# Fetching an expert layer's second-half result rows rank by rank, from before its last block pairs have run

## The chip, the core and the metric

The kernel runs on one core of one Trainium2 chip. The metric is the device time of one execution in microseconds (us). The engines are named as in the profile: PE (TensorE, matrix products; PEld is its weight load), DVE (VectorE), ACT (ScalarE), POOL (GpSimd) and SP (SyncE, which here only issues transfers). Each engine runs its own list of instructions strictly in the order in which it is written; the lists meet only at semaphores.

## What is computed

Two transformer layers over x [2048 tokens, 256], each an attention with 16 heads and a mixture-of-experts layer with 64 experts of which every token uses 8. The attention is not touched by the change except for some added transfers. The expert layer, cut to what matters:

```python
logits = x @ gate_w.T
topv, topi = jax.lax.top_k(logits, TOP_K)          # 8 of 64 experts for each token
rw = jax.nn.softmax(topv)
inter = silu(gate) * up                            # of the chosen experts
out = sum over the 8 chosen e of rw[e] * (inter[e] @ dp_w[e].T)
x = x + out + sh_g * sh_out                        # sh: a shared expert
```

The order in which the eight products of a token are added is free within rounding.

## The kernel before

**The tokens of an expert layer are worked in two halves** of 1024 (`HALVES`: tiles 8 to 15 of 128 tokens first, then tiles 0 to 7). A half has 8192 pairs of a token and an expert. They are sorted by expert into blocks of 128 rows, each block belonging to one expert, with 128 blocks for a half so that it fits whatever the routing; two blocks are a "pair", so a half is 64 pairs (`NPAIR`) and the layer 128 (`PAIRS`).

**The work of a pair n.** ACT copies the block's expert weights from `weights` to `fetched` ("fetch"); from pair 32 (`OTHER_FROM`) on DVE copies the second block's ("other"). PE multiplies (`gate_up`, L1393), ACT takes the silu (L1170), DVE the product with the other branch (L1858, two instructions), PE multiplies again (`down`, L1410), ACT moves the result out of its banks into one of two buffers `outs` (L1176), and SP writes that 256 KB to `expert_rows` in memory (L811). ACT waits before L1176 for the write of two pairs earlier (`outs_out`).

**Where tokens come from.** POOL issues all gathers of a layer in one list, `for m in range(GATHERS)`, 4 times 64 of 128 rows of 1 KB each, through `ring`, five buffers: 64 gathers of the first half's tokens, 64 of the second half's, which ACT lays down transposed in `tokensT`, then 64 gathers of result rows of the first half and 64 of the second (L1009). Result gather n serves one token tile t and one rank k: for each of 128 tokens the row that its k-th row number (`rows_of`) names. DVE multiplies it by the token's weight and adds it to x ("combine", L1872), in the order t by t, all 8 ranks of a tile one after the other. A gather waits until the combine five before it has emptied its buffer (`combined`). The ranks come from an instruction that takes the 8 largest of a token's row numbers, largest first: rank 0 is a token's last row in the blocks' order, rank 7 its first.

**What starts the result gathers.** The first gather of a half waits for the writes of all 64 pairs of that half. So the first half's gathers can run beside the second half's pairs, and the second half's cannot start before the last pair is written. DVE's combines of the second half come after its last work on the pairs.

**What sets the order.** `expert_plan` is a small planner: it has a stream of items for each kind of work with a cost and what each needs, always takes the item that could start first, and gives PE, ACT and DVE their lists. POOL's list is written by hand. Between tiles POOL computes the standard deviations for the next layer's normalisation (`inverse_std`, L947 and L949) when DVE has the statistics of a block of four tiles; DVE then writes the normalised tiles `xn` (L1903), which PE transposes (L1437) when the next phase begins. At that boundary SP loads the second layer's weights `w_raw` (L850), and POOL splits them.

**The attention before it** (`core_plan`) has 16 blocks; at the end of each ACT copies sums (L1234), and for each SP issues four small transfers of maxima (neg_hi, neg_lo) that the next products wait for.

## Time and profile before

| | us |
|---|---|
| median of 3 runs | 2178.72 |
| lowest and highest | 2177.01, 2202.41 |
| the profiled execution, its device time | 2182.6 |
| its span in the profile | 2179.9 |
| first attention | about 0 to 562 |
| first expert layer | about 562 to 1080 |
| second attention | about 1080 to 1700 |
| second expert layer | about 1700 to 2180 |

How to read it: the span is the profile's own measure of the core from first to last instruction; the device time lies 2.7 us above it. Busy times can lie beside each other, since the engines run at once. An instruction's idle time is what its engine waited just before it, with the engine or transfer that ended the wait. Over the span PE is busy 79%, DVE 69%, ACT 51% and POOL 32%.

### The profile page before, as it was taken

How to read it: one execution, taken by the hardware profiler on the slowest of the kernel's cores; microseconds unless marked ns; L12 is line 12 of the kernel's file. 1: busy time of each engine (PE TensorE's matmuls, PEld its weight loads, DVE VectorE, ACT ScalarE, POOL GpSimd, SP SyncE). 2: the span in 40 equal slices, each digit the busy share in tenths (PEclk: the TensorE clock that was granted, in tenths of full speed). 3: DMA queues.
4: the chain of work that ended last, by engine and by line, in shares of the span. 5: the costliest groups of instructions: out<-in, count | busy, mean ns of one | idle time of the engine just before them, and what ended most of it. 6: DMA issues, size and time to landing. Idle time of an engine off the chain costs nothing.

```text
span 2179.9 us, 36690 instructions
## 1 busy us (share of the span) xinstructions
PE 1716.5 (79%) x12464; PEld 1102.6 (51%) x12464; DVE 1501.5 (69%) x3241; ACT 1108.9 (51%) x1975; POOL 703.5 (32%) x778
## 2 busy tenths in 40 slices
PE   5799999999767777991096999999997677778920
PEld 4545454445545666771074454544456455667720
DVE  6588888884676834884555788888853777438843
ACT  2145858566355655760041457485672456556710
POOL 5000101001266454446740001010011564545456
PEclk9778989899879988995595679797896799999965
DMA  4640314000444544664235402231004345446643
GB/s 151 138 63 2 44 19 51 11 2 2 174 158 140 168 151 151 209 192 127 82 113 101 60 2 34 28 38 23 2 2 167 113 141 168 156 148 198 212 139 115
DMA packets 123276, 217.59 MB, mean 100 GB/s; under 512 B 16380, under 2 KB 92044, under 8 KB 118812
## 3 DMA queue, kind: packets, MB, share of 16 engines
q1 hardware_dynamic: 98520, 148.10, 25.1%
q0 software_dynamic: 24576, 67.14, 11.2%
q8 instruction: 106, 1.74, 0.4%
q14 instruction: 74, 0.61, 0.1%
HBM read 124.20 MB, written 90.46 MB: 98 GB/s over the span
## 4 chain that ended last, share of the span: by engine, by line
PE 55%; DVE 13%; POOL 7%; DMA 7%; issue 7%; ACT 5%; another core or an unknown queue 4%; SPq 1%; DVEq 0%; ACTq 0%; POOLq 0%
PE late_banks L1575 13%; PE late_banks L1533 11%; PE exp_banks L1561 7%; PE late_banks L1393 7%; POOL ring_t L1009 5%; PE exp_banks L1410 4%; DMA expert_rows<-outs_t 4%; PE late_banks L1426 3%; PE late_banks L1368 3%; DVE chunk_max_t L1974 3%; PE late_banks L1539 2%; PE exp_banks L1426 2%; DVE hot_t L1688 2%; DVE inter_t L1858 1%
## 5 line engine op out<-in xcount | busy, mean ns | idle before, releaser
L1225 ACT ACTIVATE probs_t<-exp_banks 128x1024 f32<-128x1024 f32 (+3 forms) x640 | 538.9, 896 | 348.1 <-PE exp_banks L1561 346.9
L1974 DVE TENSOR_REDUCE chunk_max_t<-late_banks 128x1 f32<-128x512 f32 (+1 forms) x960 | 603.0, 683 | 110.8 <-PE late_banks L1533 89.4
L1084 POOL TENSOR_SCALAR_AFFINE_SELECT probs_t<-probs_t 128x512 f32<-128x512 f32 x128 | 81.6, 638 | 873.0 <-ACT probs_t L1225 873.0
L1393 PE MATMUL late_banks<-tokensT_t,fetched_t 128*128 x2048 | 311.2, 298 | 26.0 <-ACT fetched_t L1153 14.0
L1575 PE MATMUL late_banks<-probs_t,values_t 128*32 128x512 f32 (+3 forms) x2560 | 322.1, 579 | 9.9 <-POOL probs_t L1084 9.5
L1004 POOL DMA_INDIRECT ring_t<-token_rows,index_t x256 | 255.4, 998 | 206.2 <-PE late_banks L1368 130.1
L1009 POOL DMA_INDIRECT ring_t<-expert_rows,rows_of_t x256 | 244.3, 954 | 201.9 <-DVE x_sb_t L1872 112.5
L1393 PEld LDWEIGHTS late_banks<-tokensT_t,fetched_t 128*128 128x128 f32 x2048 | 267.7, 204 | 58.2 <-issue 44.2
L1858 DVE TENSOR_TENSOR inter_t<-late_banks,silu_t 64x256 f32<-64x256 f32 x512 | 217.5, 425 | 103.3 <-ACT silu_t L1170 55.1
L1533 PE MATMUL late_banks<-contextT_t,Qp_t 50*128 50x512 f32 (+7 forms) x640 | 247.5, 531 | 23.9 <-DVE part_lo_t L1915 11.8
L1410 PE MATMUL exp_banks<-fetched_t,inter_t 64*128 64x128 f32 x2048 | 194.6, 311 | 41.3 <-DVE inter_t L1858 22.7
L1533 PE MATMUL late_banks<-Kp_t,Qp_t 50*128 50x512 f32 (+7 forms) x640 | 224.0, 474 | 1.9 <-DVE chunk_max_t L1974 0.9
L1176 ACT ACTIVATE outs_t<-exp_banks 128x512 f32<-128x512 f32 x256 | 152.3, 595 | 114.5 <-PE exp_banks L1410 41.6
L1872 DVE SCALAR_TENSOR_TENSOR x_sb_t<-ring_t,row_top_t,x_sb_t 128x256 f32<-128x256 f32 x256 | 122.4, 478 | 113.6 <-DMA ring_t<-expert_rows,rows_of_t 100.9
L1533 PEld LDWEIGHTS late_banks<-contextT_t,Qp_t 50*128 50x128 f32 (+1 forms) x640 | 117.8, 230 | 143.8 <-DVE chunk_max_t L1974 95.2
L1410 PEld LDWEIGHTS exp_banks<-fetched_t,inter_t 64*128 64x128 f32 x2048 | 143.7, 198 | 81.2 <-DVE inter_t L1858 34.5
L1533 PEld LDWEIGHTS late_banks<-Kp_t,Qp_t 50*128 50x128 f32 (+1 forms) x640 | 105.6, 205 | 131.4 <-DVE chunk_max_t L1974 99.3
L1848 DVE COPY fetched_t<-weights_t 128x384 f32 x192 | 84.1, 438 | 120.4 <-PE exp_banks L1410 56.3
L1153 ACT ACTIVATE fetched_t<-weights_t 128x384 f32 x320 | 158.9, 519 | 14.4 <-issue 12.7
L1561 PE MATMUL exp_banks<-Qp_t,contextT_t 52*128 52x512 f32 (+7 forms) x640 | 150.4, 442 | 15.6 <-DMA Qp_t<-neg_lo_t 11.7
L1368 PE MATMUL late_banks<-ident_t,ring_t 128*128 128x128 f32 x512 | 103.3, 312 | 75.4 <-ACT tokensT_t L1163 47.9
L1561 PE MATMUL exp_banks<-Qp_t,Kp_t 52*128 52x512 f32 (+7 forms) x640 | 148.4, 429 | 6.8 <-ACT probs_t L1225 4.8
(222 smaller groups left out, 2007.7 us busy)
## 6 DMA issues: line engine op xcount, KB each, us to landing
expert_rows<-outs_t SPq DMA_DIRECT2D x256, 256.0 KB
weights_t<-in_experts SPq DMA_DIRECT2D x8, 1728.0 KB, 13.8
Qp_t<-q_parts SPq DMA_DIRECT2D x36, 256.0 KB
weights_t<-in_experts SPq DMA_DIRECT2D x4, 2112.0 KB, 9.7
Kp_t<-k_parts SPq DMA_DIRECT2D x24, 256.0 KB
q_parts<-part_hi_t SPq DMA_DIRECT2D x16, 256.0 KB, 2.6
q_parts<-part_lo_t SPq DMA_DIRECT2D x16, 256.0 KB, 3.2
k_parts<-part_hi_t SPq DMA_DIRECT2D x16, 256.0 KB, 3.2
```

The source lines that it names most:

```text
L1004: pool.indirect_dma_start(ring[:, slot, :], None, token_rows[f][:, :], bass.IndirectOffsetOnAxis(ap=index[h][:, n:n + 1], axis=0))\
L1009: pool.indirect_dma_start(ring[:, slot, :], None, expert_rows[f][h][:, :], bass.IndirectOffsetOnAxis(ap=rows_of[:, t, k:k + 1], axis=0))\
L1153: act.activation(fetched[:, n % NFETCH, blk, :], weights[:, bass.ds(fetches[n][blk], EW)], ACT.Copy)\
L1225: act.activation(probs[:, e % NP, 2 * p:2 * p + 2, off:QB], exp_banks[sq % 2][:, :, off:QB], ACT.Exp, scale=D ** -0.5).then_inc(exp_done, 1)
L1368: last = pe.transpose(bank[:, k * P:(k + 1) * P], ring[:, slot, k * P:(k + 1) * P], ident[:, :])
L1393: last = pe.matmul(bank[:, blk * P:(blk + 1) * P], fetched[:, n % NFETCH, blk, k * P:(k + 1) * P], tokensT[:, bass.ds(starts_of[n][blk] + ...
L1410: last = pe.matmul(down_bank(n, side)[:, blk * P:(blk + 1) * P], inter[rows, n % 2, blk * P:(blk + 1) * P], fetched[rows, n % NFETCH, blk, ...
L1533: last = pe.matmul(bank[:, begin:end], Qp[s][rows, p, t * P:(t + 1) * P], Kp[s][rows, p, c * QB:c * QB + end - begin], start=True, stop=c < b)
L1561: last = pe.matmul(exp_banks[sq % 2][:, hh, off:QB], Kp[s][rows, p, j * P:(j + 1) * P], Qp[s][rows, p, b * QB + off:(b + 1) * QB], start=T ...
L1575: last = pe.matmul(pv_banks[n % NPV][32 * h:32 * h + 32, off:QB], values[:, j, GH * g + h, :], probs[:, e % NP, h, off:QB], start=(j == 0) ...
L1858: dve.tensor_tensor(inter[side * EI:(side + 1) * EI, n % 2, :], up, silu[0:EI, n % 2, :], ALU.mult)\
L1974: op = dve.tensor_reduce(chunk_max[:, slot, p, r, c], bank[:, 0:n].rearrange("q (p k) -> q p k", p=len(parts)), AX.X, ALU.max)
```

## The change

1. The shared list on POOL loses its last 64 gathers (`GATHERS = 3 * NG`). They come in a list of their own, `LATE`: first ranks 7 to 3, each for all eight tiles (40 gathers), then ranks 2 to 0 for tiles 0 to 3 and for tiles 4 to 7 (24).
2. They land in `tokensT` (the last in `ring`), in places that the pairs have read by then: late gather i waits for the product `gate_up` of pair 96 + i // 2. There is no waiting for a combine between them.
3. A rank k of the first five waits for as many writes as the furthest row of that rank needs: `marks`, 8 numbers that DVE and PE work out from the row numbers (one transpose, one product, six small DVE instructions), and that POOL reads into registers. The 41st gather waits for all writes.
4. DVE combines them after its last work on the pairs, after normalising the first half's tiles, by groups of four gathers (one semaphore for four), each tile's ranks now eight or four instructions apart.
5. In the second half ACT copies both blocks' weights for every third pair (`BOTH_EVERY`), DVE the second block's for the other two. The planner no longer has the late combines, and has the row numbers and marks earlier in DVE's list; pair 21's `down` waits for the marks.
6. Both layers' second-half results lie in one tensor, `last_rows_out`, which ACT fills during the first attention with 16 transfers of 1 MB, one after each block's sums; SP waits for them before the expert layer's loads.
7. The second layer's weights are loaded after the 26th late combine, no longer after the last pair, and POOL splits them after the last combine.

```diff
-GATHERS = 4 * NG
+GATHERS = 3 * NG
+LATE_STEP, LATE_GROUP, LOADED_FROM = 3, 4, 26
...
+BOTH_EVERY = 3
...
+def both_copied(n):
+
+    return n < OTHER_FROM or n >= NPAIR and n % BOTH_EVERY == 0
+
+
+def late_order():
+
+    order = [(t, k) for k in range(TOPK - 1, LATE_STEP - 1, -1) for t in HALVES[1]]
+    for b in range(HT // TPB):
+        order += [(t, k) for k in range(LATE_STEP - 1, -1, -1) for t in HALVES[1][b * TPB:(b + 1) * TPB]]
+    return order
+
...
-    map_steps += [("index_out", 1), ("places", 1), ("table_out", 1)]
-    pieces = [("shares", 0)]
-    for h in range(2):
-        pieces += [("rows", h)] + [("weights", i) for i in range(h * PIECES, (h + 1) * PIECES)]
+    map_steps += [("index_out", 1), ("places", 1), ("table_out", 1), ("rows", 1), ("last_rows", 1), ("marks", 1)]
+    pieces = [("shares", 0), ("rows", 0)] + [("weights", i) for i in range(2 * PIECES)]
...
-               ("dve", [("other", n) for n in pairs if n >= OTHER_FROM]),
-               ("dve", [("combine", n) for n in range(2 * NG)]),
+               ("dve", [("other", n) for n in pairs if not both_copied(n)]),
+               ("dve", [("combine", n) for n in range(NG)]),
...
-                yield "table_out", 1, 0.0
+                yield "marks", 1, 0.0
...
-        expert_rows = [[nc.dram_tensor(f"expert_rows{f}{h}", [NBLK * P, E], F32).ap() for h in range(2)] for f in range(2)]
+        last_rows_out = nc.dram_tensor("last_rows_out", [NBLK * P, E], F32).ap()
...
+        def late_tile(i):
+
+            at = i % KC * (SLOTS + P) + i // KC * E
+            return tokensT[:, at:at + E] if i < NG - 1 else ring[:, 0, :]
...
+            sp.wait_ge(rows_set, 16 * len(BLOCKS))
...
-                    sp.wait_ge(down_done, layer * PAIRS)
+                    sp.wait_ge(combined, layer * 2 * NG - NG + LOADED_FROM)
...
+            pool.wait_ge(rows_ready, 2 * f + 2)
...
+            pool.wait_ge(marked, f + 1)
...
+            written = [*low_marks, *high_marks]
+            for i, (t, k) in enumerate(LATE):
+                if i in LATE_NORMS:
+                    inverse_std(pool, norm_of["f", f] + 1, LATE_NORMS[i])
+                pool.wait_ge(gate_up_done, f * PAIRS + NPAIR + NPAIR // 2 + i // 2 + 1)
+                if i == NG - 1:
+                    pool.wait_ge(combined, f * 2 * NG + NG)
+                if i < (TOPK - LATE_STEP) * HT:
+                    if i % HT == 0:
+                        for out in outs_out:
+                            pool.wait_ge(out, written[k])
+                elif i == (TOPK - LATE_STEP) * HT:
+                    for out in outs_out:
+                        pool.wait_ge(out, 16 * ((f + 1) * PAIRS // NOUT))
+                pool.indirect_dma_start(late_tile(i), None, expert_rows[f][1][:, :],
+                                        bass.IndirectOffsetOnAxis(ap=rows_of[:, t, k:k + 1], axis=0))\
+                    .then_inc(late_in[i // LATE_GROUP], 16)
+            for place in range(2, NB):
                 inverse_std(pool, norm_of["f", f] + 1, place)
 
...
+                if layer == 1:
+                    pool.wait_ge(combined, layer * 2 * NG)
...
-                    for blk in range(2 if n < OTHER_FROM else 1):
+                    for blk in range(2 if both_copied(n) else 1):
...
+                        if layer == 0:
+                            rows = slice(n * NBLK * P // len(BLOCKS), (n + 1) * NBLK * P // len(BLOCKS))
+                            act.dma_start(last_rows_out[rows, :].rearrange("(p r) e -> p (r e)", p=P),
+                                          values[:, 0:TPB, :, :].rearrange("p t h d -> p (t h d)")).then_inc(rows_set, 16)
...
+                        pe.wait_ge(mark_step, 5 * f + 3)
...
-                    if n == NG + 16:
-                        dve.wait_ge(down_done, (f + 1) * PAIRS)
-                        for b in MIDDLE[0:2]:
-                            normalise(phase, b)
+            dve.wait_ge(down_done, (f + 1) * PAIRS)
+            for b in MIDDLE[0:2]:
+                normalise(phase, b)
+            dve.wait_ge(weights_done, 2 * f + 2)
+            last = {}
+            for i, (t, k) in enumerate(LATE):
+                n = f * 2 * NG + NG + i
+                if i % LATE_GROUP == 0:
+                    dve.wait_ge(late_in[i // LATE_GROUP], 16 * LATE_GROUP * (f + 1))
+                if t in last:
+                    dve.wait_ge(combined, last[t])
+                dve.scalar_tensor_tensor(out=x[:, t, :], in0=late_tile(i), scalar=weight8[:, t, k:k + 1],
+                                         in1=x[:, t, :], op0=ALU.mult, op1=ALU.add).then_inc(combined, 1)
+                last[t] = n + 1
+                if k == 0 and t % TPB == TPB - 1:
+                    dve.wait_ge(combined, n + 1)
+                    statistics(phase, t // TPB)
```

**POOL's list where the second half's results are gathered** (first expert layer). Before, the second half's gathers follow the first half's in the ring, with the two lines of a standard deviation between them:

```order
L1009 DMA ring_t<-expert_rows,rows_of_t 128x256 [waits combined] x59
L1009 DMA ring_t<-expert_rows,rows_of_t 128x256 [waits outs_out1,combined,outs_out0,rows_ready]
L1009 DMA ring_t<-expert_rows,rows_of_t 128x256 [waits combined] x7
L947 TENSOR_SCALAR var_eps_t<-mean_var_t 128x4 [waits aggr_done]
L949 TENSOR_TENSOR rstd_t<-var_eps_t,minus_half_t 128x4 [waits eps_done]
L1009 DMA ring_t<-expert_rows,rows_of_t 128x256 [waits combined] x4
L947 TENSOR_SCALAR var_eps_t<-mean_var_t 128x4 [waits aggr_done]
L949 TENSOR_TENSOR rstd_t<-var_eps_t,minus_half_t 128x4 [waits eps_done]
L1009 DMA ring_t<-expert_rows,rows_of_t 128x256 [waits combined] x32
L947 TENSOR_SCALAR var_eps_t<-mean_var_t 128x4 [waits aggr_done]
```

Of the change, the same place: the 64 first-half gathers stay, the register loads follow, and the late gathers wait for pairs (`gate_up_done`) and not for combines.

```order
L1056 DMA ring_t<-expert_rows,rows_of_t 128x256 [waits combined] x59
L1061 TENSOR_LOAD silu_t [waits marked,rows_ready]
L1064 TENSOR_LOAD silu_t
L1081 DMA tokensT_t<-last_rows_out,rows_of_t 128x256 [waits outs_out1,outs_out0,gate_up_done]
...
L1081 DMA tokensT_t<-last_rows_out,rows_of_t 128x256 [waits outs_out1,outs_out0,gate_up_done]
L1081 DMA tokensT_t<-last_rows_out,rows_of_t 128x256 [waits gate_up_done] x22
L1081 DMA ring_t<-last_rows_out,rows_of_t 128x256 [waits combined,gate_up_done]
L997 TENSOR_SCALAR var_eps_t<-mean_var_t 128x4 [waits aggr_done]
```

What moved: nothing of the second half waits behind a combine any more, except its last gather; two of the four standard deviations now stand behind all gathers.

**DVE's list early in the second half** (about pairs 70 to 73; L1858 of before and L1977 of the change are the pair's product, COPY the weight copy, SCALAR_TENSOR_TENSOR the combine). Before, a copy and one combine stand between two products:

```order
L1872 SCALAR_TENSOR_TENSOR x_sb_t<-ring_t,row_top_t,x_sb_t 128x256
L1858 TENSOR_TENSOR inter_t<-late_banks,silu_t 64x256 x2
L1843 TENSOR_LOAD silu_t
L1848 ISA
L1848 COPY fetched_t<-weights_t 128x384
L1872 SCALAR_TENSOR_TENSOR x_sb_t<-ring_t,row_top_t,x_sb_t 128x256
L1858 TENSOR_TENSOR inter_t<-late_banks,silu_t 64x256 x2
L1848 ISA
L1848 COPY fetched_t<-weights_t 128x384
L1872 SCALAR_TENSOR_TENSOR x_sb_t<-ring_t,row_top_t,x_sb_t 128x256
L1858 TENSOR_TENSOR inter_t<-late_banks,silu_t 64x256 x2
```

Of the change, five combines and two copies stand in three pairs:

```order
L1977 TENSOR_TENSOR inter_t<-late_banks,silu_t 64x256 x2
L1967 ISA
L1967 COPY fetched_t<-weights_t 128x384
L1991 SCALAR_TENSOR_TENSOR x_sb_t<-ring_t,row_top_t,x_sb_t 128x256 x2
L1977 TENSOR_TENSOR inter_t<-late_banks,silu_t 64x256 x2
L1991 SCALAR_TENSOR_TENSOR x_sb_t<-ring_t,row_top_t,x_sb_t 128x256 x2
L1962 TENSOR_LOAD silu_t
L1967 ISA
L1967 COPY fetched_t<-weights_t 128x384
L1977 TENSOR_TENSOR inter_t<-late_banks,silu_t 64x256 x2
L1991 SCALAR_TENSOR_TENSOR x_sb_t<-ring_t,row_top_t,x_sb_t 128x256
L1977 TENSOR_TENSOR inter_t<-late_banks,silu_t 64x256 x2
```

What moved: the first half's 64 combines are spread over pairs 68 to 107, where they were spread over pairs 68 to 128.

**DVE's list at the end of the first expert layer.** Before:

```order
L1895 BN_AGGR mean_var_t<-stats_t 128x2 x4
L1872 SCALAR_TENSOR_TENSOR x_sb_t<-ring_t,row_top_t,x_sb_t 128x256 x17
L1903 TENSOR_SCALAR xn_t<-x_sb_t,mean_var_t,rstd_t 128x256 x8
L1872 SCALAR_TENSOR_TENSOR x_sb_t<-ring_t,row_top_t,x_sb_t 128x256 x15
L1892 BN_STATS stats_t<-x_sb_t 128x6 x4
L1895 BN_AGGR mean_var_t<-stats_t 128x2 x4
L1872 SCALAR_TENSOR_TENSOR x_sb_t<-ring_t,row_top_t,x_sb_t 128x256 x32
L1892 BN_STATS stats_t<-x_sb_t 128x6 x4
L1895 BN_AGGR mean_var_t<-stats_t 128x2 x4
L1903 TENSOR_SCALAR xn_t<-x_sb_t,mean_var_t,rstd_t 128x256 x8
```

Of the change (L2007 is the late combine, L2035 the normalisation of eight tiles, L2024 and L2027 the statistics):

```order
L1967 COPY fetched_t<-weights_t 128x384
L1977 TENSOR_TENSOR inter_t<-late_banks,silu_t 64x256 x6
L2035 TENSOR_SCALAR xn_t<-x_sb_t,mean_var_t,rstd_t 128x256 x8
L2007 SCALAR_TENSOR_TENSOR x_sb_t<-tokensT_t,row_top_t,x_sb_t 128x256 x52
L2024 BN_STATS stats_t<-x_sb_t 128x6 x4
L2027 BN_AGGR mean_var_t<-stats_t 128x2 x4
L2007 SCALAR_TENSOR_TENSOR x_sb_t<-tokensT_t,row_top_t,x_sb_t 128x256 x11
L2007 SCALAR_TENSOR_TENSOR x_sb_t<-ring_t,row_top_t,x_sb_t 128x256
L2024 BN_STATS stats_t<-x_sb_t 128x6 x4
L2027 BN_AGGR mean_var_t<-stats_t 128x2 x4
L2035 TENSOR_SCALAR xn_t<-x_sb_t,mean_var_t,rstd_t 128x256 x8
L2045 TENSOR_TENSOR xT_t<-exp_banks,xT_t 128x512 x4
L2045 TENSOR_TENSOR xT_t<-late_banks,xT_t 128x512 x4
```

What moved: the first half's normalisation stands ahead of all 64 late combines, and no combine of them stands beside a pair.

## Rows read from the trace of the kernel before

**Rows 1.** Busy time and rates by stretch; share of DMA engines and GB/s last.

```profile
core 0: us, PE busy (x) PEld busy (x) DVE busy (x) ACT busy (x) POOL busy (x), PEclk, DMA share, GB/s
100.00:560.00 460.00, 440.24 (x3194) 218.43 (x3191) 368.82 (x709) 277.75 (x340) 43.31 (x68) 0.88 0.17 23
1160.00:1700.00 540.00, 509.68 (x3448) 262.20 (x3448) 407.37 (x834) 295.85 (x376) 53.91 (x88) 0.82 0.23 41
857.00:978.00 121.00, 107.29 (x928) 90.86 (x928) 99.06 (x241) 78.44 (x174) 60.96 (x64) 0.94 0.64 196
990.00:1075.00 85.00, 3.67 (x16) 3.27 (x16) 34.12 (x78) 2.40 (x4) 65.36 (x70) 0.52 0.37 113
```

**Rows 2.** One line's instructions (ns min/median/max, first and last start): gathers, four stretches; DVE's copy.

```profile
L1009 POOL DMA_INDIRECT ring_t<-expert_rows,rows_of_t x64: 943/947/1142, 857.4 to 977.2; - x64
...
L1009 POOL DMA_INDIRECT ring_t<-expert_rows,rows_of_t x64: 945/949/1170, 990.4 to 1074.3; - x64
...
L1009 POOL DMA_INDIRECT ring_t<-expert_rows,rows_of_t x64: 943/947/1141, 1964.3 to 2082.2; - x64
...
L1009 POOL DMA_INDIRECT ring_t<-expert_rows,rows_of_t x64: 945/949/959, 2093.4 to 2172.4; - x64
...
L1848 DVE COPY fetched_t<-weights_t x60: 360/472/572, 857.8 to 980.8; 128x384 f32 x60
```

**Rows 3.** The silu, one for each pair, in four stretches of second halves.

```profile
L1170 ACT ACTIVATE silu_t<-late_banks x40: 360/378/380, 858.2 to 940.1; 64x256 f32<-64x256 f32 x40
...
L1170 ACT ACTIVATE silu_t<-late_banks x21: 362/378/379, 941.8 to 982.9; 64x256 f32<-64x256 f32 x21
...
L1170 ACT ACTIVATE silu_t<-late_banks x39: 361/378/379, 1968.5 to 2042.7; 64x256 f32<-64x256 f32 x39
...
L1170 ACT ACTIVATE silu_t<-late_banks x22: 360/378/380, 2042.7 to 2087.6; 64x256 f32<-64x256 f32 x22
```

**Rows 4.** Groups by line, 870 to 977 us: busy us, mean ns, idle before, releasers.

```profile
L1858 DVE TENSOR_TENSOR inter_t<-late_banks,silu_t 64x256 f32<-64x256 f32 x108 | 45.9, 425 | 13.1 <-ACT silu_t L1170 9.3 <-issue 1.9
L1176 ACT ACTIVATE outs_t<-exp_banks 128x512 f32<-128x512 f32 x54 | 32.2, 596 | 27.6 <-DMA expert_rows<-outs_t 15.5 <-PE exp_banks L1410 10.1 <-issue 1.9
L1872 DVE SCALAR_TENSOR_TENSOR x_sb_t<-ring_t,row_top_t,x_sb_t 128x256 f32<-128x256 f32 x55 | 25.8, 470 | 0.1
```

**Rows 5.** Timeline (start, us, engine, line), end of the first expert layer, then of the second.

```profile
1016.78 2.67 DVE L1903 TENSOR_SCALAR xn_t<-x_sb_t,mean_var_t,rstd_t 128x256 f32<-128x256 f32 x8
...
1077.04 0.48 DVE L1872 SCALAR_TENSOR_TENSOR x_sb_t<-ring_t,row_top_t,x_sb_t 128x256 f32<-128x256 f32 x1 [0.83 <-DMA ring_t<-expert_rows,rows_of_t]
1077.56 1.41 DVE L1892 BATCH_NORM_STATS2 stats_t<-x_sb_t 128x6 f32<-128x256 f32 x4
...
2175.19 0.49 DVE L1872 SCALAR_TENSOR_TENSOR x_sb_t<-ring_t,row_top_t,x_sb_t 128x256 f32<-128x256 f32 x1 [0.80 <-DMA ring_t<-expert_rows,rows_of_t]
```

**Rows 6.** The chain of waits, pieces in order of time: writes of result rows.

```profile
941.35 4.64 DMA expert_rows<-outs_t
...
987.38 2.20 DMA expert_rows<-outs_t
```

**Rows 7.** DMA queues, 857 to 978 us: packets, MB, share of 16 engines.

```profile
q1 hardware_dynamic: 15840, 15.27, 36.5%
q0 software_dynamic: 3024, 8.26, 26.8%
```

**Rows 8.** Who waited for whom, first attention, 100 to 560 us: total, times, longest.

```profile
PEld exp_banks L1561 <- DMA Qp_t<-neg_lo_t: 6.8, 6, 3.0
```

**Rows 9.** Lines at the end of the first attention, and a load of 1216 KB.

```profile
L1234 ACT ACTIVATE sums_t<-late_banks x3: 597/602/603, 517.1 to 550.4; 128x512 f32<-128x512 f32 x3
...
L789 SPq DMA_DIRECT2D g_raw_t<-in_router x1: 357/357/357, 562.5 to 562.5; - x1
...
L850 SPq DMA_DIRECT2D w_raw_t<-in_w_b x1: 467/467/467, 987.8 to 987.8; - x1
...
DMA to landing us min/median/max: 6.2/6.2/6.2
```

122 lines of the change are left out of this document (94 added, 28 removed).

## The prediction

> **What bounds the kernel now.** I began with the busy times by stretch [rows 1]. In the two attentions PE works nearly all the time (440 of 460 us, 510 of 540), so nothing can be won or lost there except through PE. In the second half of the first expert layer's pairs, 857 to 978 us, PE is busy 107 of 121 us. Then come 85 us, 990 to 1075, in which PE works 4 us and POOL 65. That is the stretch the change is about; the second layer ends with one like it.
>
> The gathers of result rows [rows 2] show its shape. The first half's 64 start between 857.4 and 977.2, one every 1.90 us, because each waits for a combine, and there is one combine to a pair. The second half's 64 start between 990.4 and 1074.3. In the second layer, where no standard deviation stands between them, the same 64 go from 2093.4 to 2172.4: 79.0 / 63 = 1.254 us each, of which 0.949 is the instruction. That is POOL at its own pace. In the first layer they take 83.9 us, so three standard deviations cost 4.9, or 1.6 each. After the last gather's start, 2.8 us pass to its combine, then the statistics follow [rows 5].
>
> The silu, one for each pair, gives the pairs' pace [rows 3]: 81.9 us over 39 steps (2.10 us) in the first part of the half, 41.1 over 20 (2.06) in the last; in the second layer 74.2 / 38 = 1.95 and 44.9 / 21 = 2.14. What holds it above PE's work is the write of results: ACT waited 15.5 of its 27.6 idle us for it [rows 4], and on the chain a write takes 2.20 us when nothing runs beside it and up to 4.64 when much does [rows 6]. With two buffers that decides every second pair.
>
> **The sum, first layer.** The gathers of the second half no longer start at 990.4 but as soon as POOL is through with the first half's. (a) *First-half gathers.* In the new order DVE has five combines in three pairs, so POOL's own pace asks for 1.254 x 5 / 3 = 2.09 us a pair. DVE's work in such a pair is 0.85 for the product, two thirds of a copy of 0.47, and 5/3 of a combine of 0.47: 0.85 + 0.31 + 0.78 = 1.94 us [rows 2, 4]. Both are near the pair's present 2.10, so nothing stretches much. The lower bound for the 64 gathers is 64 x 1.254 = 80 us, the upper one the present 120 + 1. DVE's order and POOL will not mesh perfectly; I take 86, near the lower end, since the ring of five gives 6.3 us against a landing of 2.8. (b) *Register loads.* No row has one on POOL. Between nothing and one standard deviation more than this (1.6) lies 0 to 4 us; I take 2. (c) *Late gathers.* 63 steps of 1.254 are 79.0, and two standard deviations 3.3. The last starts at 857.4 + 86 + 2 + 79.0 + 3.3 = 1027.7, against 1074.3: **46.6 us earlier**.
>
> For that, no other wait of the list may bind. *Pairs:* late gather 0 would start at 945, near pair 108 (pair 107's silu is at 941.8), and needs pair 96; then the allowance grows by two gathers a pair, POOL does 1.6. *Marks:* evaluating the reference's router, each second half fills at most 96 of its 128 blocks, and the furthest rows of ranks 7 to 3 lie in pairs 23, 35, 37, 38 and 41 of the half (second layer 23, 30, 34, 38, 41), all written before POOL asks. *All writes:* the 41st gather comes at 857.4 + 86 + 2 + 40 x 1.254 + 3.3 = 998.9; the last write lands at 987.38 + 2.20 = 989.6 today. That leaves 9.3 us. *DVE:* from 984.4 it normalises (2.67), then 64 combines at 0.48 are 30.7, two statistics 3.6: 1021.4, just ahead of POOL. So the late combines, which had lain beside the gathers, still do. The pairs' last twenty lose their combines on DVE, but gain gathers at 1.254 in place of 1.90; I let them end as before.
>
> **Second layer.** 1964.3 + 86 + 2 + 79.0 = 2131.3 against 2172.4: **41.1 us earlier**. The 41st gather is at 2102.5, the last write at about 2093: 9 us again.
>
> **What it costs.** The last group of four combines waits for its last gather and then takes four combines in place of one: 3 x 0.45, in both layers 2.7 us. The two standard deviations behind the gathers lie in the wait for the last statistics. The weights of the second attention take 6.2 us from an issue at the 26th late combine (about 1000), 25 us before POOL splits them, so they stay hidden. Marks, the transpose and the product are six small DVE instructions and two of PE in the first half, where DVE is not the bound; with pair 21's added wait I take 1 us a layer, 0 to 5. ACT copies a block more in every third pair, 0.47 / 3 = 0.16 us a pair, from 0.51 us of idle time [rows 4]; if that cover is gone it costs 64 x 0.16 = 10 us in a stretch with 9 to spare. The 16 writes of 1 MB in the first attention: 16 issues of 0.47 us are 7.5 us of ACT, which has 180 idle us there [rows 1, 9]; the transfers, 6.2 us each by the load of 1216 KB, can hold up the small transfers of maxima, for which PE waits 6.8 us in all today [rows 8]. I take 3 us, 0 to 20. The last is issued after 550.4 + 0.6 and lands near 557.5; SP's next load is at 562.5, so that wait is covered.
>
> Sum: 46.6 + 41.1 - 2.7 - 2 - 3 = 80.0 us from the profiled execution's 2182.6, that is 2102.6. It lies 3.9 us above the median of the runs, so for the median I forecast 2178.7 - 80 = **2099 us**.
>
> **The rivals.** *B, the writes bind.* In 857 to 978 us writes hold 36.5% of the DMA engines and gathers 26.8% at one per 1.90 us [rows 7]; at 1.254 the gathers' share becomes 41%, together 77%. If a pair then takes 0.3 us more over 60 pairs, the last write lands 18 us later, and the 41st gather waits some 9 us longer than it would; over two layers 2099 + 18 = 2117. For it speaks the spread of a write, 2.2 to 4.6 us [rows 6]; against it that the engines are not full, and that the pairs lose other work. The Trainium skill, "DMA: Bandwidth & Descriptors", section "Issuing engines are not separate DMA queues", says that transfers of all issuers interleave on the same 16 engines; the measured shares fit that. *C, the order does not speed the first-half gathers.* If DVE, in order behind its pairs, holds the ring to one combine per pair, the late list starts at 977.2 + 1.3 + 2, its last gather at 1062.8 (11.5 us earlier), in the second layer at 2164.5 (7.9): with the costs 2167, no change. Against it stands DVE's 22 idle us of 121 in that stretch. *D, the copies hold up the gathers.* 42 copies of a half, 0.47 us each, run beside gathers; were each added to POOL's list, 20 us a layer, the time would be 2139. Against it: gathers beside a copy in every pair have a median of 0.947 us, those beside none 0.949, while it is the copy that stretches from 0.36 to 0.57 [rows 2]. The Trainium skill, "SBUF — State Buffer", section "SBUF: two separate sides", has the rule for it: a 32-bit SBUF copy on VectorE locks GpSimd out of writing descriptors. By that rule the gathers would be the slow ones; the trace shows it hardly. *E, slower:* each 1 MB write delays the maxima of its block by its whole 6.2 us and PE has no other work; 16 x 6.2 = 99 us less the 3 taken, 2195. It decides from 5 us a write on, 80 / 16. Against it: PE has three kinds of products to choose from, and today's group loads, megabytes too, leave only those 6.8 us. *F, better:* POOL without a gap in (a) and no price for registers or writes: 12 + 4 + 5 less, 2078.
>
> **How the numbers follow.** Forecast 0.55, B 0.20, F 0.10, C 0.07, D 0.04, E 0.02, others 0.02. PE's granted clock, 0.88 and 0.82 in the attentions, moves of its own: 1% of 1000 us is 10 us, in the range. Range 2080 to 2128: the forecast, B and most of F. A change of 2% is 44 us (about what a measurement of this kernel can tell from none), so faster is below 2135: forecast, B, F and half of what remains, 0.88; within 2%: 0.10; slower: 0.02.
>
> **What would show it.** Of the changed kernel: 64 gathers from `expert_rows` in 80 to 92 us (119.8 to 121 is C); 64 from `last_rows_out` with hardly a gap; no pause before the 41st (a pause named after the writes is B); gathers still 0.95 us (longer is D); waits for neg_lo under 10 us in the first attention (tens are E); and from the last write to the last gather's start 38 us, no longer 85. The forecast is wrong if POOL waits for DVE or for a pair in the late list, or if the last pair ends over 9 us later.

## The result and the profile after

The change made the kernel slower.

| | median, us | range, us | ratio to before (95%) |
|---|---|---|---|
| before | 2180.5 | 2177.0 to 2202.4 | |
| changed | 2244.9 | 2228.3 to 2257.5 | 1.026 (1.021 to 1.032) |
| forecast | 2099 | 2080 to 2128 | 0.963 |

The profiled execution of the changed kernel took 2257.5 us (span 2255.4), 75 us more than that of before. Its lines have moved: silu L1244, copy of a result on ACT L1250, gate_up L1481, down L1499, first-half gathers L1056, late gathers L1081, late combines L2007, result writes on SP L858, 1 MB writes L1311.

Busy time and rates by stretch (the first answers to the third of [rows 1]; the others are pieces of the second half and of what follows it):

```profile
core 0: us, PE busy (x) PEld busy (x) DVE busy (x) ACT busy (x) POOL busy (x), PEclk, DMA share, GB/s
857.00:978.00 121.00, 89.83 (x708) 75.30 (x708) 74.06 (x182) 64.19 (x150) 62.80 (x63) 0.88 0.52 163
...
1003.00:1031.00 28.00, 8.18 (x40) 7.04 (x40) 3.19 (x8) 4.35 (x11) 18.02 (x19) 0.50 0.40 118
1031.00:1062.00 31.00, 27.94 (x242) 23.47 (x240) 15.60 (x39) 21.02 (x47) 5.77 (x6) 0.93 0.48 157
1068.00:1082.00 14.00, 0.00 (x0) 0.00 (x0) 12.73 (x33) 0.27 (x1) 13.70 (x2) 0.50 0.32 118
```

PE is busy 90 us in the stretch where it had been busy 107 of 121, and then comes a stretch of 28 us in which it works 8 while POOL issues 19 gathers. The gathers and the pairs (count, ns min/median/max, first and last start; they answer to [rows 2, 3]):

```profile
L1056 POOL DMA_INDIRECT ring_t<-expert_rows,rows_of_t x64: 943/949/1199, 870.3 to 979.9; - x64
...
L1081 POOL DMA_INDIRECT tokensT_t<-last_rows_out,rows_of_t x63: 943/949/13933, 981.2 to 1108.7; - x63
L1081 POOL DMA_INDIRECT ring_t<-last_rows_out,rows_of_t x1: 949/949/949, 1110.0 to 1110.0; - x1
...
  DMA last_rows_out<-outs_t: 28.0, 2
...
L1244 ACT ACTIVATE silu_t<-late_banks x39: 362/377/378, 871.7 to 982.8; 64x256 f32<-64x256 f32 x39
...
L1244 ACT ACTIVATE silu_t<-late_banks x23: 362/377/378, 982.8 to 1060.1; 64x256 f32<-64x256 f32 x23
```

The first half's gathers take 109.6 us (120 before, 86 forecast). A pair takes 111.1 / 38 = 2.92 us in the first part and 77.3 / 22 = 3.51 in the last, where it took 2.10 and 2.06. The last silu comes 77 us later than before, and POOL waits 28 us for the last writes. One late gather takes 13.93 us. The last gather of the layer starts at 1110.0, 36 us later than before; the second layer repeats all of it (last gather 2247.7, before 2172.4).

What a slow stretch looks like, from the timeline (start, us, engine, line; in brackets the idle time before and its releaser):

```profile
1009.83 2.07 PE L1481 MATMUL late_banks<-tokensT_t,fetched_t 128*128 x8
1010.80 0.95 POOL L1081 DMA_INDIRECT tokensT_t<-last_rows_out,rows_of_t  x1 [0.30 <-issue]
...
1015.94 0.38 ACT L1244 ACTIVATE silu_t<-late_banks 64x256 f32<-64x256 f32 x1 [7.56 <-issue]
...
1017.29 1.23 PE L1499 MATMUL exp_banks<-fetched_t,inter_t 64*128 64x128 f32 x8 [5.38 <-DVE inter_t L1977]
1018.32 0.95 POOL L1081 DMA_INDIRECT tokensT_t<-last_rows_out,rows_of_t  x1 [0.30 <-issue]
...
1027.93 0.60 ACT L1250 ACTIVATE outs_t<-exp_banks 128x512 f32<-128x512 f32 x1 [11.62 <-remote]
1028.03 0.36 DVE L1967 COPY fetched_t<-weights_t 128x384 f32 x1 [10.79 <-remote]
1028.26 0.95 POOL L1081 DMA_INDIRECT tokensT_t<-last_rows_out,rows_of_t  x1 [3.98 <-remote]
```

PE ends gate_up at 1011.9, and ACT, idle for 7.56 us, starts its silu 4.0 us after that. PE ends down at 1018.5, and ACT starts the copy 9.4 us after that, at the same moment at which DVE gets its word from PE. POOL has issued 17 gathers at its full pace since 1003.3. Its burst ends at 1024.3, because the next gather waits for a signal of PE too; the held signals all come through 3.6 us later. What PE tells the other engines arrives late; what ACT and DVE tell others does not: PE's down at 1017.29 starts 0.05 us after DVE's product has ended, and over all pairs from 865 to 1062 us PE never starts a down more than 0.06 us behind the product it waited for (31 times), nor DVE a product more than 0.03 us behind its silu (33 times). In the lines of waits this stands under "issue" and "remote", since the profile has no releaser for it.

The long gather, from the same timeline:

```profile
1064.81 15.92 DVE L2007 SCALAR_TENSOR_TENSOR x_sb_t<-tokensT_t,row_top_t,x_sb_t 128x256 f32<-128x256 f32 x40
...
1067.62 13.93 POOL L1081 DMA_INDIRECT tokensT_t<-last_rows_out,rows_of_t  x1 [27.68 <-DMA last_rows_out<-outs_t]
```

DVE had been kept from its late combines by the pairs; once they are through it runs 40 of them with nothing between. The 41st gather starts inside this run and ends 0.8 us after it.

What the prediction feared most was not there. In 871 to 987 us the two queues together hold less than before (53.1% of the DMA engines' time; 63.3% in [rows 7]; the gathers' own share is about the same), the wait for neg_lo is shorter than before [rows 8], and a 1 MB write costs ACT 0.33 us and lands in 4.0 (median; the longest took 19.5):

```profile
q0 software_dynamic: 3226, 8.83, 27.6%
q1 hardware_dynamic: 10608, 10.23, 25.5%
...
PEld exp_banks L1651 <- DMA Qp_t<-neg_lo_t: 5.9, 6, 1.9
...
L1311 ACTq DMA_DIRECT2D last_rows_out<-values_t x16: 326/326/353, 105.3 to 556.6; - x16
...
DMA to landing us min/median/max: 3.8/4.0/19.5
```

Two theories came out of this. **T1:** while POOL issues gathers back to back, the completion signals of PE reach the other engines late, and the pairs slow down. **T2:** DVE's run of combines, which read two operands from SBUF each, locks POOL out of its gather.

Two measures are used below. *Late records*: increments by PE that the trace records over 0.8 us after the end of the instruction they belong to. They show where something is late, but overstate how much (the record of the gate_up above stands at 1028.0, yet ACT had started on it at 1015.9). *ACT behind PE*: for each silu and each copy of a result, the time from the end of the product it reads, or of ACT's previous instruction if that is later, to its start, summed. That is time in which ACT stood. A copy can also stand for the write that still empties its buffer, so the part that ends with a landing of that write is given apart. Landings are recorded only in part in some traces (more on that below), so that part is a lower bound there.

### The profile page after: what moved, and what is told of

The parts are those of the page before. It is cut to its first block, busy times and chain, and to the rows that moved or that the text cites. A ratio compares the mean times of both kernels' runs of the same rounds, so it can differ in the third digit from the quotient of the medians.

```text
span 2255.4 us, 36670 instructions
## 1 busy us (share of the span) xinstructions
PE 1774.7 (79%) x12470; PEld 1142.7 (51%) x12470; DVE 1477.0 (65%) x3211; ACT 1123.3 (50%) x2017; POOL 739.6 (33%) x778
## 4 chain that ended last, share of the span: by engine, by line
PE 56%; DVE 15%; issue 7%; another core or an unknown queue 6%; POOL 5%; DMA 4%; ACT 4%; SPq 1%; DVEq 1%; ACTq 0%; POOLq 0%
PE late_banks L1665 12%; PE late_banks L1623 10%; PE late_banks L1481 8%; PE exp_banks L1651 7%; PE exp_banks L1499 6%; POOL tokensT_t L1081 3%; DVE chunk_max_t L2106 3%; PE late_banks L1516 3%; DVE inter_t L1977 3%; PE late_banks L1456 2%; PE late_banks L1629 2%; PE exp_banks L1516 2%; DVE hot_t L1778 2%; ACT probs_t L1299 1%
## 5 line engine op out<-in xcount | busy, mean ns | idle before, releaser
L1481 PE MATMUL late_banks<-tokensT_t,fetched_t 128*128 x2048 | 335.6, 315 | 56.9 <-ACT fetched_t L1227 40.7
L1665 PE MATMUL late_banks<-probs_t,values_t 128*32 128x512 f32 (+3 forms) x2560 | 330.4, 593 | 9.9 <-POOL probs_t L1158 9.5
L1481 PEld LDWEIGHTS late_banks<-tokensT_t,fetched_t 128*128 128x128 f32 x2048 | 291.1, 219 | 88.8 <-issue 77.6
L1977 DVE TENSOR_TENSOR inter_t<-late_banks,silu_t 64x256 f32<-64x256 f32 x512 | 217.6, 425 | 170.9 <-ACT silu_t L1244 101.6
L1499 PE MATMUL exp_banks<-fetched_t,inter_t 64*128 64x128 f32 x2048 | 208.5, 328 | 108.0 <-DVE inter_t L1977 76.4
L1250 ACT ACTIVATE outs_t<-exp_banks 128x512 f32<-128x512 f32 x256 | 152.0, 594 | 170.0 <-PE exp_banks L1499 79.5
L1499 PEld LDWEIGHTS exp_banks<-fetched_t,inter_t 64*128 64x128 f32 x2048 | 154.9, 213 | 154.2 <-DVE inter_t L1977 96.8
L1081 POOL DMA_INDIRECT tokensT_t<-last_rows_out,rows_of_t x126 | 147.0, 1167 | 106.2 <-DMA last_rows_out<-outs_t 55.3
L1967 DVE COPY fetched_t<-weights_t 128x384 f32 x150 | 57.0, 380 | 190.6 <-PE exp_banks L1499 94.3
L1227 ACT ACTIVATE fetched_t<-weights_t 128x384 f32 x362 | 175.6, 516 | 10.9 <-issue 10.5
L1244 ACT ACTIVATE silu_t<-late_banks 64x256 f32<-64x256 f32 x256 | 95.3, 372 | 141.4 <-PE late_banks L1481 72.8
L1056 POOL DMA_INDIRECT ring_t<-expert_rows,rows_of_t x128 | 128.0, 1000 | 113.8 <-DVE x_sb_t L1991 60.4
```

Source lines behind the costliest of these rows:

```text
L1081: pool.indirect_dma_start(late_tile(i), None, expert_rows[f][1][:, :], bass.IndirectOffsetOnAxis(ap=rows_of[:, t, k:k + 1], axis=0))\
L1227: act.activation(fetched[:, n % NFETCH, blk, :], weights[:, bass.ds(fetches[n][blk], EW)], ACT.Copy)\
L1250: act.activation(outs[:, out % NOUT, :, :].rearrange("p b (s c) -> p s b c", s=2), down_banks(n).rearrange("p s (b c) -> p s b c", b=2), A ...
L1481: last = pe.matmul(bank[:, blk * P:(blk + 1) * P], fetched[:, n % NFETCH, blk, k * P:(k + 1) * P], tokensT[:, bass.ds(starts_of[n][blk] + ...
L1499: last = pe.matmul(down_bank(n, side)[:, blk * P:(blk + 1) * P], inter[rows, n % 2, blk * P:(blk + 1) * P], fetched[rows, n % NFETCH, blk, ...
L1665: last = pe.matmul(pv_banks[n % NPV][32 * h:32 * h + 32, off:QB], values[:, j, GH * g + h, :], probs[:, e % NP, h, off:QB], start=(j == 0) ...
```

## The experiments

### First group: the two theories one at a time (before: 2186.8 us)

**Serial combines.** Each late combine also waits for the one before it:

```diff
-                if t in last:
-                    dve.wait_ge(combined, last[t])
+                dve.wait_ge(combined, n)
```

> The changed kernel, in which each late combine on DVE also waits for the combine before it (a semaphore of its own), so that DVE no longer issues a run of 40 combines with nothing between them. Theory T2 (the run of combines, each with two SBUF inputs, locks the 41st late gather out: it takes 13.93 us in layer 1 and 13.25 us in layer 2 where the others take 0.95): the 41st gather takes under 2 us, the last gather of each layer comes 10 to 13 us earlier, and the time falls from 2245 to 2215-2230 us. Rival (the long gather has another cause: a full queue after 40 gathers, or the transfers of the last writes): it stays near 13 us and the time does not fall, or rises by the waits. The pairs stay as slow as in the changed kernel in both theories (last silu of the first layer near 1060).

2200.4 us, ratio 1.007 (1.003 to 1.011). The long gather is gone in both layers (longest 1.82 us), the last silu is about where it was (1057.4), and the last gather follows it by 36.3 us instead of 49.9.

**No late gather before the last write.** The first late gather waits for all writes:

```diff
-                if i < (TOPK - LATE_STEP) * HT:
-                    if i % HT == 0:
-                        for out in outs_out:
-                            pool.wait_ge(out, written[k])
-                elif i == (TOPK - LATE_STEP) * HT:
+                if i == 0:
```

> The changed kernel, in which no late gather is issued before the last row of the second half is written: the first late gather waits for all writes. Theory T1 (gathers issued one behind the other hold up PE's completion signals, and so the pairs beside them): the first-half gathers, in bursts of four to seven, still slow pairs 67 to 106 (2.9 us a pair), but the last 21 pairs run without gathers at about 2.0 us each, so that the last silu of the first layer comes near 1025 instead of 1060; the 64 late gathers follow at 1.25 us, 80 us, and the last starts near 1112, as in the changed kernel (1110): a time within 1% of its 2245 us. Rival (the pairs are slow for another reason that is there without late gathers too: DVE's new order, the every-third-pair copy on ACT): the last 21 pairs stay near 3.7 us each, the last silu near 1058, and the time is near 2320 us.

2233.5 us, 1.022 (1.015 to 1.030). The silu up to the end of the first half's gathers, and those after it:

```profile
L1240 ACT ACTIVATE silu_t<-late_banks x41: 360/377/377, 859.8 to 974.1; 64x256 f32<-64x256 f32 x41
...
L1240 ACT ACTIVATE silu_t<-late_banks x22: 361/377/377, 976.4 to 1017.0; 64x256 f32<-64x256 f32 x22
```

Without gathers beside them a pair takes 40.6 / 21 = 1.93 us instead of 3.51; beside the first half's gathers it still takes 2.86. ACT behind PE falls to 1.4 us over the 43 instructions from 974 to 1015 us, none over 0.05, and PE's granted clock rises from 0.89 (861 to 974 us) to 0.98 (974 to 1017). So the gathers beside the pairs slowed them, and starting them early gained nothing here.

**Pauses.** Two memsets of 128x64 on POOL behind each first-half result gather and the first 20 late ones:

```diff
+            for _ in range(PAUSES):
+                if pauses[0]:
+                    pool.wait_ge(paused, pauses[0])
+                pool.memset(pause_tile[:, :], 0.0).then_inc(paused, 1)
+                pauses[0] += 1
```

> The changed kernel, with a pause on POOL (two memsets of 128x64, one behind the other, some 0.4 us) behind each result gather of the first half and each of the first 20 late ones. Nothing else changes: same gathers, bytes, order, writes. Theory T1 (PE's signals are held while POOL issues gathers back to back, and released in a gap): with the gaps the held signals go, pairs 67 to 127 run near 2.1 us each instead of 2.9, the last silu of the first layer comes near 1000-1015 instead of 1060, and though POOL does more, the time falls to 2150-2200 us. Rival (the pairs are slowed by the load on the DMA queues, or by DVE's order): the pause moves nothing but the gathers, the pairs stay at 2.7 us and more, and the time stays at 2240 or rises.

2210.5 us, 1.009 (1.004 to 1.014): POOL does more, and the kernel is 1.7% faster than the changed one. But the gathers came 1.48 us apart, not far enough: 26 records of PE in 97 us are still late, by 1.6 us on average and 2.95 at most, pairs 67 to 106 still take 2.63 us each, and the last silu comes at 1042, not at 1000 to 1015. In both layers the 41st gather is long (14.35 and 13.26 us). Right in direction, too small in size.

**Pauses in the kernel before.** Three memsets behind each token gather from the 17th on:

> The kernel before, with a pause on POOL (three memsets of 128x64, some 0.6 us) behind each token gather from the 17th on; these gathers come in bursts of four beside the pairs (1.3 to 3.4 us of held signals in each of 11 bursts between 714 and 857). Theory T1: the bursts are spaced, the holds of that stretch (80 us over 165 signals) go, a pair takes 1.85-2.0 us instead of 2.06, and the time falls by 5 to 25 us to 2155-2175. Rival (signals in the bursts are late because of the transfers or for nothing that binds): no change, 2175-2185, or slower by the 60 us that POOL is paused where POOL binds.

2201.3 us, 1.008 (1.005 to 1.012), slower. Of the late records of the token stage (628 to 852 us: 70 before, 119 us in sum) 6 are left, 9 us in sum, so the gaps do what T1 says of the records, and ACT behind PE falls from 29.5 to 11.7 us over the stage, of which 4.7 is for writes. But a pair there needs two token gathers, and these now come 1.69 us apart or more by the pauses themselves; the stage takes 11 us longer. Where POOL is the bound, spacing buys nothing.

### Second group: a surprise (before: 2096.6 us)

**One combine per pair.** `BOTH_EVERY = 1000` in place of 3 in the changed kernel, so that DVE copies for every pair again and the planner gives it one combine a pair.

> The changed kernel with its every-third-pair copy on ACT taken back (from pair 32 on, DVE copies the second half of every pair's weights, as in the kernel before). The planner then gives DVE one combine of the first half per pair, in the order of the kernel before, instead of five in three pairs; the late gathers by rank, their marks and the 1 MB writes stay. Theory T1 (what slows the pairs is gathers issued back to back beside them; they came in bursts because five combines in three pairs asked for them): the first-half gathers stand alone again (1.85 us apart), pairs 67 to 127 take 2.0 to 2.15 us, the last silu comes 130 us after the 65th pair's, as before, few late gathers run beside pairs, and the time is within 1% of the kernel before, 2165-2205 us. Rival (the slow pairs come from what stayed: the late scheme, its register loads, the longer DVE stream or the writes): pairs 67 to 106 stay near 2.9 us and the time stays above 2220.

**Thin gathers.** In the kernel before, in the place of the pauses:

```diff
+            pool.indirect_dma_start(thin_tile[:, thins[0] % 4, :], None,
+                                    token_rows[f][:, :].rearrange("s (a c) -> (s a) c", c=THIN),
+                                    bass.IndirectOffsetOnAxis(ap=index[h][:, n:n + 1], axis=0)).then_inc(...)
```

> The kernel before, where behind each token gather from the 17th on POOL issues a further gather of 128 rows of 64 bytes (16 floats, into a tile that nothing reads), in the place of the pause of the run with pauses on the token gathers. It moves 1/32 of the bytes of a token gather, and keeps POOL issuing gathers at 1.25 us one behind the other. There, with pauses, 6 of 204 signals of PE were held over 0.8 us between the first and the 65th pair, 9 us in sum. Theory T1a (it is the issuing of gathers, their descriptors, that holds the signals, not their bytes): held signals come back, over 100 us in sum in that stretch and in long runs, and the pairs take 2.5 us or more instead of 2.06: a time of 2260 us and more. Theory T1b (it is the bytes in flight): the sum stays under 30 us and the time near the 2201 us of the run with pauses, plus at most the 0.5 us per gather that the extra ones are longer than the pauses.

**Wide pauses**, three memsets, with serial combines:

> The changed kernel with serial late combines (each waits for the one before it) and with a pause of three memsets behind each first-half result gather and the first 16 late ones: gathers 1.7 us apart or more, where two memsets gave 1.48 us and left 26 signals held by 1 to 2 us in 97 us. DVE keeps its order of five combines in three pairs. Theory T1 (held signals are what slows the pairs): in the run with three memsets behind the token gathers nothing was held, so nothing is here; pairs 67 to 106 take 2.1 to 2.25 us instead of 2.9, the last silu comes 135 to 145 us after the 65th pair's instead of 193, and the time is 2165-2195 us. Rival (DVE's order of combines in bunches, or the load on the transfers, slows the pairs): without held signals the pairs still take 2.6 us or more, and the time is 2200 or more.

**A planner that spaces the combines**, `"gather": 1.9` in its costs, with serial combines:

> The changed kernel with serial late combines, where the planner is told that a gather takes 1.9 us instead of 1.25: it then gives DVE four combines in three pairs instead of five, and starts them ten pairs later; eleven of them stand behind the last pair. No pause on POOL. Theory T1: ring slots come free one at a time for most gathers, so these are 1.5 to 1.9 us apart and hold little; pairs 67 to 106 take 2.1 to 2.4 us, and the time is 2170-2200 us, under the 2200 of the changed kernel with serial combines alone. Rival (the sum of the work beside the pairs decides, not its bunches): pairs 67 to 106 slow down by what the gathers beside them are, the late gathers behind them take what was saved, and the time is 2200 or more.

| | us | ratio to before |
|---|---|---|
| one per pair | 2080.3 | 0.989 (0.983 to 0.995) |
| thin gathers | 2346.7 | 1.119 (1.111 to 1.128) |
| wide pauses | 2106.2 | 1.001 (0.996 to 1.005) |
| planned wide | 2103.5 | 1.002 (0.999 to 1.006) |

The kernel before itself ran 4% faster here than in the first group, and in all four traces not one increment of PE is recorded over 0.8 us late, not even beside 42 token gathers with POOL's usual 0.30 us between them (one per pair, from 756.9 us). So T1 could not be tested by the thin gathers, and the wide pauses failed for a plain reason: with five combines in three pairs and gathers 1.68 us apart or more, a pair cannot take less than 5 x 1.68 / 3 = 2.8 us, and it took 2.8. The spaced planner did keep the pairs at 2.03 us, but its first half's gathers start 22 us behind the 65th silu and end behind the last one (971.8 and 964.6 us), so the last gather comes 91.3 us after the last silu, as before (91.4): nothing is gained. T1 as I had written it (gathers always hold the signals) was wrong: there is a state in which they don't. The question became what the changed kernel does in that state.

### Third and fourth group: the changed kernel in both states, on one chip

> The changed kernel itself, with nothing edited, once more. In the runs so far PE's completion signals were held for microseconds beside gathers in every trace of before, of the changed kernel and of the first four experiments, all with before near 2180-2187 us; in the four experiments of the second group, with before at 2097 us, no signal of 500 was held over 0.4 us, even beside 52 gathers in a row. Theory T1 in the form that this leaves (the holds are a state of the chip that the program meets; where they are, gathers issued back to back slow the pairs, where they are not, they don't): if before runs near 2180 here, signals are held and the changed kernel is 2 to 3.5% slower; if before runs near 2100, nothing is held, pairs 67 to 106 take about 2.1 us instead of 2.9, and the changed kernel is 1 to 4% faster, by the sum of the prediction less the 41st gather's 13 us. Rival (the changed kernel's own order makes it slow everywhere): 2 to 3% slower than before whatever before's time is.

> The changed kernel with serial late combines, the same kernel as the first experiment, now beside the changed kernel on one chip, so that the cost of the 41st gather (13.93 and 13.25 us) is measured without the difference between two chips. Theory T2 (DVE's run of combines locks POOL out): 12 to 27 us faster than the changed kernel of this group, the 41st gather at 0.95 us, if DVE falls behind the gathers here too; if the pairs end before the late gathers do, DVE keeps pace and there is no run of 40: then neither kernel has a long gather and they take the same time within 0.5%. Rival (what made the first experiment 2% faster than the changed kernel was the chip): no difference even where the long gather is there.

> The changed kernel with DVE copying for every pair again, one combine per pair, as in the fifth experiment, beside the changed kernel on one chip. If signals are held here (before near 2180): the first-half gathers stand alone and hold nothing, the pairs keep 2.05-2.15 us, and it is within 1% of before, 2165-2200, and 2 to 3% faster than the changed kernel. If nothing is held (before near 2100): about 1% faster than before, as measured (0.989), and slower than the changed kernel by the 10 to 30 us per layer that five combines in three pairs save in the first half's gathers (120 us at one per pair, 80 at POOL's own pace).

| third group (before 2186.2) | us | ratio to before |
|---|---|---|
| changed | 2239.3 | 1.026 (1.016 to 1.035) |
| serial combines | 2198.6 | 1.005 (1.000 to 1.010) |
| one per pair | 2167.6 | medians 0.991, no interval |

Signals were late again (43 late records in the changed kernel's second half), and the changed kernel was slow again. Serial combines gain 41 us beside it, of which the two long gathers (15.89 and 13.26 us) explain 27; the rest is of the size by which single executions differ. In the one-per-pair kernel a long gather of 13.10 us stands in the second layer, again inside a DVE run of 40 combines (15.93 us). Behind it lies the longest held signal of all traces:

```profile
2091.88 1.23 PE L1499 MATMUL exp_banks<-fetched_t,inter_t 64*128 64x128 f32 x8 [10.60 <-issue]
...
2122.25 0.95 POOL L1081 DMA_INDIRECT tokensT_t<-last_rows_out,rows_of_t  x1 [0.30 <-issue]
2128.31 0.60 ACT L1250 ACTIVATE outs_t<-exp_banks 128x512 f32<-128x512 f32 x1 [19.00 <-remote]
...
2128.37 15.93 DVE L2007 SCALAR_TENSOR_TENSOR x_sb_t<-tokensT_t,row_top_t,x_sb_t 128x256 f32<-128x256 f32 x40 [36.03 <-issue]
```

PE ends the layer's last product at 2093.1. POOL issues 24 more gathers, and ACT and DVE hear of it 35 us later. The burst ends because the 41st gather waits for the last write, which ACT cannot even prepare, and 5 us after its end the signal comes through. So one combine per pair does not protect the last pairs: the late gathers beside them still run back to back. (This profiled execution took 16 us more than the kernel's median; in the first layer ACT was 0.6 us behind at the same place.)

Then the same chip came up once more, with before at 2093.1 us:

> The changed kernel with both edits that gave something: one combine of the first half per pair (DVE copies for every pair again) and late combines that each wait for the one before. Theories T1 and T2 together: as the one-per-pair kernel (0.989 and about 0.991 of before), without the long 41st gather where that came up (13.1 us in its second layer in the last group, none in the group before): 0.980 to 0.990 of before, so faster than both kernels of the case. Rival (the serial waits cost what the lockout costs, or the lockout is rare): 0.990 to 0.995, no better than one per pair alone.

> The kernel with a thin gather (128 rows of 64 bytes) behind each token gather once more, since the chip that it ran on held no signal in any kernel. If signals are held here in the kernels beside it: theory T1a (issuing gathers back to back holds them, whatever their bytes): over 100 us held in sum in the token stage of layer 1, most signals of PE there held, holds of 5 us and more, and the ratio to before above 1.12. Theory T1b (bytes in flight hold them): under 30 us in sum, since full gathers start 2.5 us apart, and the ratio stays near the 1.119 that POOL's doubled issuing costs by itself.

> The changed kernel, nothing edited, for the two theories on why it is slow. If before runs near 2180 here and signals are held: 2 to 3.5% slower for the third time. If before runs near 2100 and no signal is held (the state in which this kernel has not run yet): theory T1 says pairs 67 to 106 at 2.1 us, the first half's gathers in 80-90 us and the time 1 to 4% below before; the rival (its order makes it slow everywhere) says 2 to 3% above before.

| fourth group (before 2093.1) | us | ratio to before |
|---|---|---|
| changed | 2052.1 | 0.981 (0.972 to 0.991) |
| one per pair and serial | 2081.7 | 0.994 (0.991 to 0.997) |
| thin gathers | 2335.8 | 1.116 (1.107 to 1.125) |

The same kernel on the same chip is 2.6% slower than before in one group and 1.9% faster in the other. The traces of its second half, first the third group's, stretch, first-half gathers and what they waited for:

```profile
873.00:983.00 110.00, 81.38 (x622) 68.34 (x620) 70.49 (x172) 56.70 (x130) 65.30 (x67) 0.86 0.56 170
...
L1056 POOL DMA_INDIRECT ring_t<-expert_rows,rows_of_t x64: 945/949/1191, 872.3 to 979.1; - x64
...
  DVE x_sb_t L1991: 28.0, 15
...
ACT silu_t L1244 <- PE late_banks L1481: 14.3, 11, 3.3
...
L1244 ACT ACTIVATE silu_t<-late_banks x41: 363/377/378, 870.1 to 982.7; 64x256 f32<-64x256 f32 x41
```

and the fourth group's:

```profile
838.00:923.00 85.00, 70.86 (x624) 59.38 (x624) 69.46 (x173) 57.69 (x130) 63.35 (x65) 0.98 0.73 219
923.00:965.00 42.00, 37.17 (x336) 31.32 (x336) 25.95 (x68) 29.99 (x70) 32.56 (x36) 1.00 0.76 228
...
L1056 POOL DMA_INDIRECT ring_t<-expert_rows,rows_of_t x64: 941/946/1182, 838.3 to 921.2; - x64
...
  DVE x_sb_t L1991: 6.4, 15
...
ACT silu_t L1244 <- PE late_banks L1481: 2.5, 7, 1.0
...
L1081 POOL DMA_INDIRECT tokensT_t<-last_rows_out,rows_of_t x63: 942/946/14272, 922.5 to 1017.2; - x63
...
L1244 ACT ACTIVATE silu_t<-late_banks x41: 359/377/378, 836.1 to 922.8; 64x256 f32<-64x256 f32 x41
```

The same 41 silus take 86.7 us instead of 112.6 (2.17 and 2.82 us a pair) and the 64 gathers 82.9 instead of 106.8, with *more* bytes a second (219 against 170 GB/s). That rules out the load on the DMA engines. Of the 25 us by which the third group's stretch is longer, PE stands idle in 14.5 and is busy in 10.5 more with the same products, at a granted clock of 0.86 instead of 0.98. The low clock is not a property of the state: in the run whose late gathers wait for all writes, in the first group, it was 0.98 again as soon as there were no gathers beside the pairs. ACT behind PE, over the same instructions, and the late records:

| | stretch, us | instructions | ACT behind PE, us | of it for writes | over 0.8 us | late records |
|---|---|---|---|---|---|---|
| changed, third group | 873 to 983 | 77 | 38.8 | 0.0 | 18 | with the next row 43 |
| | 983 to 1057 | 42 | 34.4 | 0.3 | 9 | |
| changed, fourth group | 838 to 922 | 77 | 5.2 | 2.7 | 1 | 0 |
| | 922 to 965 | 42 | 5.0 | 3.6 | 2 | 0 |
| before (case) | 857 to 978 | 116 | 23.7 | 9.9 | 7 | 5 |
| one per pair and serial, fifth | 863 to 985 | 121 | 24.3 | 11.6 | 8 | 8 |
| one per pair and serial, fourth | 836 to 949 | 119 | 16.6 | 12.2 | 4 | 0 |

In the first stretch ACT lost 34 us more behind PE, and the silus took 26 us longer. Gathers that stand alone in the second half suffer much less: the kernel with one combine per pair and serial combines, which has a trace in both states, takes 2.03 us a pair in the fifth group and 1.88 in the fourth:

```profile
L1244 ACT ACTIVATE silu_t<-late_banks x65: 359/377/379, 830.8 to 950.8; 64x256 f32<-64x256 f32 x65
```

That is 8% against 30% in the changed kernel. What decides is the state together with gathers back to back beside the pairs. The same two traces show where a kernel whose result gathers stand alone loses its 4%; the kernel before has no trace in the state in which signals are in time. Of the 84 us between them, 59 lie in the first 64 pairs of the two layers (220.9 and 215.8 us against 187.9 and 190.0), where token gathers come in bursts, and 14 in the second halves.

### Fifth group: issuing or bytes (before: 2180.0 us)

> The changed kernel with serial late combines, for the third time. If no signal is held here (before near 2095): the changed kernel alone was 0.9815 of before there, with a 41st or 42nd gather of 14.27 and 11.18 us; theory T2 takes both away, so 0.968 to 0.974 of before (2027-2040 us), the fastest kernel of the case. Rival (with DVE nearly keeping pace the lockout was hidden behind the last combines): 0.980 as before. If signals are held (before near 2185): 1.005 as in the two groups of such a state.

> One combine per pair and serial late combines together, again. Where no signal is held it was 0.9937 of before. If signals are held here (before near 2185): gathers beside the pairs stand alone and hold few signals, the long gather (13.1 us in one layer of the one-per-pair kernel, which took 2168 beside 2186) is gone, so 0.980 to 0.992 of before, faster than both kernels in that state. Rival: the lockout was chance and the gain of one per pair was noise: 0.995 to 1.005.

> The kernel with a thin gather (128 rows of 64 bytes) behind each token gather. Where no signal is held it took 1.119 and 1.116 of before, the price of POOL's doubled issuing. If signals are held here: theory T1a (issuing gathers back to back holds them, whatever their bytes): over 100 us held in sum in the token stage of layer 1, holds of 5 us and more. Theory T1b (the bytes in flight hold them): under 30 us in sum, and 1.11 to 1.12 of before.

| | us | ratio to before |
|---|---|---|
| serial combines | 2205.6 | 1.009 (1.005 to 1.012) |
| one per pair and serial | 2164.1 | 0.992 (0.988 to 0.996) |
| thin gathers | 2474.2 | 1.134 (1.128 to 1.140) |

Signals were late here. The kernel with thin gathers has the same code as in the fourth group; up to its 64th silu it shows 120 late records, 498 us in sum and up to 10.9 us, where the kernel before has 70 and 119 us, the kernel with pauses 6 and 9 us, and the fourth group 0. ACT behind PE is 91.8 us over 127 instructions, against 4.3 over 126 there, and the first 64 pairs take 374.8 us against 314.3. The waits, 700 to 1000 us (total, times, longest):

```profile
DVE fetched_t L1864 <- remote: 101.7, 16, 8.2
ACT tokensT_t L1179 <- remote: 71.9, 16, 7.5
...
ACT outs_t L1192 <- remote: 57.8, 15, 8.1
...
L961 POOL DMA_INDIRECT thin_t<-token_rows,index_t x93 | 88.7, 953 | 30.1 <-issue 30.1
```

A thin gather moves 8 KB, 1/16 of a full one's 128 (the expectations say 1/32), and the bytes move more slowly, since a full gather now starts every 2.5 us at best. On the gathers' DMA queue this run has 7440 packets and 12.96 MB in 300 us (700 to 1000), the run with pauses 3888 and 10.62 in 160 (700 to 860): as many packets a microsecond (24.8 and 24.3) and fewer bytes (43 and 66 KB). A gather starts every 1.63 us on average here and every 1.98 there, but here 154 of the 184 come without a gap, there none. So it is the issuing of gathers, one right behind the other, that makes PE's signals late, not what they move: T1a. Whether POOL's work on a gather does it or the signals that each gather brings of its own was not separated. A thin gather takes POOL 0.953 us, as long as one of 1 KB rows.

One combine per pair with serial combines is faster than before in both states, and as fast as anything measured where signals are late; its pairs and late gathers there:

```profile
L1244 ACT ACTIVATE silu_t<-late_banks x62: 360/377/379, 862.7 to 986.8; 64x256 f32<-64x256 f32 x62
...
L1081 POOL DMA_INDIRECT tokensT_t<-last_rows_out,rows_of_t x63: 942/947/1237, 983.3 to 1065.2; - x63
```

A pair takes 124.1 / 61 = 2.03 us, and the late gathers start 1.8 us behind the first half's last one and run without a gap; in the kernel before that step took 13.2 us, the wait for the last write [rows 2]. It is the only part of the change that survives where signals are late. Where they are not, the changed kernel is faster still (0.981); with serial combines it should gain the 13.3 and 10.2 us of its two long gathers more, which was not measured: the serial kernel met the late state in all three of its runs. For the one-per-pair kernel this sum did not come: 0.980 to 0.990 was expected of it with serial combines in the fourth group, and it took 0.994, no better than one per pair alone (0.989, on another chip), which had no long gather there.

## Why the prediction was wrong

**"Pairs: I let them end as before"** is the step that failed. Everything else leant on it: the 41st gather was to come 9.3 us after the last write; the last write came 77 us later than before, and POOL waited 28 us for it. The prediction named the condition ("wrong if the last pair ends over 9 us later"), but gave it no mechanism beyond a load on the writes. I had read a pair's pace off DVE's and POOL's work and left out how the engines tell each other that work is done. The rows had a hint: before the change the result gathers stand alone, one every 1.90 us, in just the stretch where pairs keep 2.10 us, so the trace of before showed nothing of gathers back to back beside pairs of this stage. Its token stage had it, in bursts of four, and I had not looked there: ACT stood 29.5 us behind PE in 628 to 852 us.

**(a) First-half gathers**, forecast 86 us: 109.6 in the case, 82.9 and 81.1 in the fourth group. The working (POOL's pace and DVE's 1.94 us meet near 2.09 a pair) holds where signals are in time. Where they are late, DVE gets silu and product late, its combines behind them free the ring late, POOL stands 28 us (third group), and then issues the next burst.

**(b) Register loads**, forecast 2 us: the first late gather starts 1.3 us behind the last of the first half, that is at POOL's own pace. They cost nothing.

**(c) Late gathers**, forecast 82.3 us from first to last: 128.8 in the case, of which 28.0 are waits for writes, 13.0 the long gather and 4.0 a gap named "remote". In the fourth group 96.1, of which 13.3 are the long gather; the rest, 82.8, is the forecast.

**"DVE, just ahead of POOL"** in the late list failed too, by one row: DVE starts the list only after the last pairs, with 40 combines ready. Rival D (DVE locks POOL out) was the right mechanism with the wrong instruction; I had tied it to the copies and dismissed it by the gathers' median of 0.947 us, which stayed right (0.949 beside copies). The Trainium skill has the rule that fits, in "SBUF — State Buffer", section "Who interferes with whom": a DVE instruction with two SBUF inputs contends with a GpSimd instruction that reads SBUF, and the one that is first blocks the other. A combine has two, and a gather reads its indices. The traces agree, and add that the block outlasted the single instruction: 11 to 16 us over a run of 36 to 40 combines of 0.40 us each, in nine layers of five traces, and never when each combine waited for the one before it (seven traces, fourteen layers, longest gather 2.0 us). But not every such run does it: in the first layers of three other traces (the late gathers behind all writes, one per pair in the second and in the third group) DVE runs 12 combines without a gap, and the twelve gathers that start inside these runs take 0.95 to 1.28 us. What a run needs to hold a gather is open.

**Rival B** (writes bind): the shares of the queues fell instead of rising, and with 228 GB/s in the fourth group the pairs take 2.02 us. Wrong. **Rival C** (first-half gathers not faster): wrong. **Rival E** (1 MB writes): the wait for neg_lo did not grow, so not by its mechanism. But over all traces the router's load at the end of the first attention is issued at 565.8 us on average without the 1 MB writes (five traces, 562.5 to 571.7) and at 574.4 with them (fourteen, 564.1 to 589.6): 8.6 us where I took 3. Which wait it is was not settled.

**The sum in the state it fits.** Forecast -80 us, measured in the fourth group -41 (-58 to -19). With the two long gathers (13.3 and 10.2 us more) and 5.6 more for the 1 MB writes, the sum would have been -80 + 23.5 + 5.6 = -51, inside that interval; but the 80 had been read off a trace with late signals, so that it fits so well is in part luck. The chances had a slip too: forecast, B, F and half of the rest are 0.925 and not 0.88. The chance of 0.02 for slower was the real fault: three of five groups, the case's own not counted, met the state in which this change loses.

## What to carry to other kernels

Work on POOL that issues indirect DMAs back to back was not free for its neighbours here even though no engine, queue or buffer was short: look first for stretches of the trace of before in which it already does, and compare how soon ACT starts on what PE has finished there and elsewhere. Do not let a run of two-operand DVE instructions on SBUF go without a wait beside gathers; where a run of 40 held a gather, a wait in each combine saved 11 to 14 us a layer, and it cost 0.4 to 0.7 us at the kernel's end (8.1 to 8.4 us instead of 7.7 from the last gather on). And where one kernel is timed in several groups, look at the time of the unchanged kernel first: a change that leans on a state of the chip can win in one and lose in the next.

## What the chip showed that I had not expected

- PE's completion signals late by 4 to 9 us beside 17 gathers issued 1.25 us apart and by 35 beside 24, within 0.05 us when POOL is silent, hardly late with gathers 1.8 us apart, and partly with 1.48. In both attentions of the kernel before, where POOL issues none, not one of some 2100 records is late. ACT's and DVE's signals were not late.
- This is there in some groups of runs and absent in others, on one and the same chip (before: 2180 to 2187 us with it, 2093 to 2097 without). What brings it about is open; the kernels were the same. It shows in the traces apart from PE too: of the 4096 increments by which the result writes tell that they have landed, the traces of the late state hold 1707 to 2197 (3046 with pauses behind the token gathers), those of the other 4022 to 4089.
- A gather of 128 rows takes POOL 0.95 us whether a row has 64 bytes or 1 KB.
- A run of 36 to 40 DVE combines without a wait held a gather for 11 to 16 us, until the run was over.
